# First attention of a four-layer MetaFormer: bias inside the score matmul, compact probabilities, product with V in 32x32 tiles

## The reference

```python
# 16 consecutive tokens form one sequence; 3 heads of 32 channels
qkv = x @ Wqkv + bqkv
q, k, v = jnp.split(qkv, 3, axis=-1)
q = q.reshape(B, G, P, H, DH) * SCALE
attn = jnp.einsum('bgihd,bgjhd->bghij', q, k)
bias = rel_table[REL_IDX].reshape(P, P, H).transpose(2, 0, 1)
attn = jax.nn.softmax(attn + bias[None, None], axis=-1)
out = jnp.einsum('bghij,bgjhd->bgihd', attn, v)
return out.reshape(B, G, P, D) @ Wm + bm
```

## Time and profile before

| what | value |
|---|---|
| runs | 892.6, 896.56, 895.98 us, median 895.98 |
| profiled execution | span 887.6 us; its own total time is not listed apart from the runs |
| TensorE busy | 789.4 us, 89% of the span |
| VectorE, GpSimd, ScalarE busy | 636.2, 563.9, 436.3 us |
| chain that ended last, whole program | TensorE 75%, VectorE 13%, issue 4%, ScalarE 3%, GpSimd 3% |
| steady part of the first attention | about 47 to 87 us of the span |

### The profile page before, as it was taken

The page is one execution under the profiler, slowest core; times in us unless marked ns, Lnnn a source line. Parts: engine busy times, 40 slices in busy tenths (PEclk is TensorE's granted clock), DMA queues, the critical chain, the costliest instruction groups (busy, mean ns, idle before and its releaser), DMA issues.

```text
span 887.6 us, 25193 instructions
## 1 busy us (share of the span) xinstructions
PE 789.4 (89%) x9360; PEld 647.9 (73%) x9360; DVE 636.2 (72%) x1699; ACT 436.3 (49%) x793; POOL 563.9 (64%) x887
## 2 busy tenths in 40 slices
PE   4778677579989999997998899999979998999996
PEld 4567465557867888885887678888868786888886
DVE  5899788658866777785778357777867774577755
ACT  1345355157755544435787354454545554445341
POOL 6443642345428788776876467887766776688765
PEclk9898778779999999998999899999988999999999
DMA  8610100000022110100001001101000001111030
GB/s 185 116 26 0 46 1 1 1 1 2 1 66 61 30 54 27 29 2 1 2 0 46 27 28 28 55 27 28 3 1 2 0 20 35 30 44 40 27 82 19
DMA packets 39515, 26.45 MB, mean 30 GB/s; under 512 B 27464, under 2 KB 32313, under 8 KB 39377
## 3 DMA queue, kind: packets, MB, share of 16 engines
q1 hardware_dynamic: 38428, 24.46, 11.0%
q10 hardware_dynamic: 998, 0.80, 0.4%
HBM read 8.33 MB, written 1.57 MB: 11 GB/s over the span
## 4 chain that ended last, share of the span: by engine, by line
PE 75%; DVE 13%; issue 4%; ACT 3%; POOL 3%; DMA 1%; ACTq 0%; DVEq 0%; POOLq 0%
PE PS L1580 21%; PE PS L1553 9%; PE PS L1554 8%; PE PS L1557 4%; PE PS L1357 3%; PE PS L1668 3%; PE PS L1655 2%; PE PS L1679 2%; PE PS L1343 2%; PE PS L1688 2%; PE PS L1345 2%; PE PS L1344 2%; PE PS L1490 2%; PE PS L1404 2%; PE PS L1698 2%
## 5 line engine op out<-in xcount | busy, mean ns | idle before, releaser
L667 ACT ACTIVATE H<-PS,B 128x512 f32<-128x512 f32 x288 | 173.7, 690 | 194.1 <-PE PS L1557 194.1
L1580 PEld LDWEIGHTS PS<-M,H 128*64 128x64 f32 x4608 | 192.3, 137 | 21.8 <-issue 15.1
L1580 PE MATMUL PS<-M,H 128*64 128x96 f32 x4608 | 205.2, 248 | 1.8 <-DVE X L1161 1.8
L1161 DVE SCALAR_TENSOR_TENSOR X<-PS,G,X 128x96 f32<-128x96 f32 (+1 forms) x384 | 121.8, 318 | 95.7 <-PE PS L1580 85.2
L465 POOL TENSOR_TENSOR msum<-stats 128x4 f32<-128x4 f32 (+1 forms) x61 | 16.0, 263 | 164.4 <-DVE stats L844 136.4
L1553 PE MATMUL PS<-XH,M1h 128*128 128x512 f32 x192 | 78.5, 409 | 0.0
L475 POOL TENSOR_TENSOR XN<-X,mean 128x384 f32<-128x384 f32 x56 | 47.1, 841 | 49.0 <-PE PS L1357 49.0
L1554 PE MATMUL PS<-FHL,M1l 128*128 128x512 f32 x192 | 76.9, 401 | 0.0
L501 POOL TENSOR_TENSOR PF<-G,B 128x1536 f32<-128x1536 f32 x24 | 66.2, 2760 | 10.2 <-DVE G L1152 10.2
L509 POOL TENSOR_TENSOR ex<-euler,dl 128x16 f32<-128x16 f32 x24 | 69.9, 2911 | 1.7 <-DVE dl L1125 1.6
L479 POOL TENSOR_TENSOR rs<-ve,half 128x4 f32<-128x4 f32 (+1 forms) x61 | 65.5, 1073 | 4.8
(11 more groups left out here) (248 smaller groups left out, 1902.7 us busy)
## 6 DMA issues: line engine op xcount, KB each, us to landing
FHL<-XH SPq DMA_DIRECT2D x36, 192.0 KB, 2.5
FHL<-XL SPq DMA_DIRECT2D x36, 64.0 KB, 2.1
X<-XH SPq DMA_DIRECT2D x12, 192.0 KB, 2.5
raw<-L_ffn_w SPq DMA_DIRECT2D x3, 576.0 KB, 4.8
M<-L_ffn_w SPq DMA_DIRECT2D x3, 576.0 KB, 6.0
X<-x SPq DMA_DIRECT2D x4, 384.0 KB, 7.9
XH<-XL SPq DMA_DIRECT2D x24, 64.0 KB, 1.9
out<-X SPq DMA_DIRECT2D x8, 192.0 KB, 2.6
```

The source lines that it names most:

```text
L667: act.activation(H[p][:, c, :], bank(UB[c]), ACT.Gelu, bias=B1[e][:, c:c + 1]).then_inc(gelu_a, 1)
L1161: ins = dve.scalar_tensor_tensor(xt(g, t), bank(4 + t % 2)[:, e * C:(e + 1) * C], G[:, t, e:e + 1], xt(g, t), ALU.mult, ALU.add)
L1580: ins = pe.matmul(Y[rows, x * C:(x + 1) * C], H[p][:, j, t * P + rows.start:t * P + rows.stop], M2[e][:, j, :], start=c == 0, stop=c == CH ...
```

## The change

- The rows 96 to 127 of qT and kT, zero before, hold an identity and the bias with the mask. The score matmul adds bias and mask itself; VectorE's addition (line 894) goes, and maximum and subtraction read PSUM. Two copies on VectorE fill these rows in the opening, and qT's are zeroed again after the phase.
- The probabilities are transposed by one 128-row instruction in place of four of 32 rows and stay compact (PA shrinks; its zeroing on GpSimd goes).
- The product with V is 48 matmuls of 32 keys by 32 channels by 32 tokens in place of 12; the keys of block q write bank q (0 to 3), and one ScalarE copy gathers the four banks.
- Banks: scores from 3 to 5, k from 1 to 4, V from 2 to 6 (shared with the output projection), and q stays in bank 0, which the product now uses too. So k comes first, q waits until OT has been copied, and V waits for the residual update of group g-1. ScalarE copies kT ahead of qT.
- In `body(7)` the product waits until the first feed-forward group has been read from banks 0 and 1, and `ffn_up(0)` waits for the OT copy of group 7.

```diff
-        PA = [hflat[1][:, o:o + HEADS * GTOK].rearrange("p (h t) -> p h t", h=HEADS) for o in (3072, 4608)]
+        PA = [hflat[1][:, o:o + GT * HEADS * 32] for o in (3072, 3456)]
...
+        KB, VB = (4, 1), (6, 2)
...
-                return PS[:, 3:4, 0:GT * HEADS * 32].rearrange("p b (u t h j) -> p (b u) t h j", u=2, t=2, h=HEADS)
+                return PS[:, 5:6, 0:GT * HEADS * 32].rearrange("p b (u t h j) -> p (b u) t h j", u=2, t=2, h=HEADS)
...
             for i in range(2):
-                ins = pool.memset(PA[i], 0.0)
-            ins.then_inc(ms_p, 1)
...
-                        act.activation(OT[0:C, :], bank(5, 512, C), ACT.Copy).then_inc(ot_a, 1)
+                        if ka == 1:
+                            act.activation(OT[0:C, :], bank(5, 512, C), ACT.Copy).then_inc(ot_a, 1)
+                        else:
+                            act.activation(OT[0:C, :].rearrange("c (t q j) -> c q t j", t=GT, q=4),
+                                           PS[0:C, 0:4, 0:GTOK // 4].rearrange("c q (t j) -> c q t j", t=GT), ACT.Copy).then_inc(ot_a, 1)
...
+                        dve.tensor_reduce(mx[:].rearrange("p (u v) -> p u v", u=2), S, AX.X, ALU.max).then_inc(mx_v, 1)
+                        dve.wait_ge(mx_v, n + 2)
                         if ka == 0:
                             after(dve, tr_v, g + 1)
-                            dve.tensor_tensor(sct, scores(0).rearrange("p u t h j -> p (u t) h j"),
-                                              BI[:].unsqueeze(1).to_broadcast([P, GT, HEADS, bs]), ALU.add).then_inc(sc_r, 1)
...
-                            for q in range(P // bs):
-                                rows = slice(q * bs, (q + 1) * bs)
-                                ins = dve.transpose(PA[1 - p][rows, :, :].rearrange("p h (t j) -> p t h j", t=GT)[:, :, :, rows],
-                                                    sct[rows])
-                            ins.then_inc(tr_v, 1)
+                            dve.transpose(PA[1 - p], SC[:, 0:GT * HEADS * bs]).then_inc(tr_v, 1)
...
+            dve.tensor_copy(qT[C:P, :].rearrange("p (r j) -> p r j", j=32), ident[C:P, C:P].unsqueeze(1).to_broadcast([P - C, GTOK // 32, 32]))
+            dve.tensor_copy(kT[C:P].rearrange("p h (r j) -> p h r j", j=32),
+                            BI[C:P].unsqueeze(2).to_broadcast([P - C, HEADS, GTOK // 32, 32])).then_inc(bias_v, 1)
...
             dve.wait_ge(xu[0], GROUPS)
-            dve.wait_ge(ms_p, 6)
+            dve.wait_ge(s_pe, GROUPS)
+            dve.memset(qT[C:P, :], 0.0).then_inc(ms_v, 1)
+            dve.wait_ge(ms_p, 5)
...
+                        elif isinstance(g, int) and g == GROUPS - 1:
+                            pe.wait_ge(fl_v, 1)
...
+                                for q in range(P // bs):
+                                    keys = slice(q * bs, (q + 1) * bs)
+                                    for h in range(HEADS):
+                                        rows = slice(h * DH, (h + 1) * DH)
+                                        ins = pe.matmul(PS[rows, q, t * bs:(t + 1) * bs], V[keys, t, rows],
+                                                        PA[p][keys, (t * HEADS + h) * bs:(t * HEADS + h + 1) * bs], start=True, stop=True)
...
+                        three(bank(KB[ka], 512, C), wh[:, C:2 * C], wl[:, C:2 * C], xh[:], xl[:]).then_inc(k_pe, 1)
+                        if ka == 0:
+                            if has(g, 0):
+                                pe.wait_ge(ot_a, n + 1)
+                            three(bank(0, 512, C), wh[:, 0:C], wl[:, 0:C], xh[:], xl[:]).then_inc(q_pe, 1)
...
+                        if ka == 0 and has(g, -1):
+                            pe.wait_ge(xu[0], g)
...
                         pe.wait_ge(wt_v, 7)
+                        pe.wait_ge(ot_a, GROUPS)
```

More of the change, by code:

```diff
@@ L549, in _ @@
             for i in range(2):
-                ins = pool.memset(PA[i], 0.0)
-            ins.then_inc(ms_p, 1)
-            for i in range(2):
                 pool.memset(BW[i][:], 0.0)
@@ L627, in body @@
                             rows = slice(h * DH, (h + 1) * DH)
-                            ins = act.activation(kT[rows, h, :], PS[rows, 1, :], ACT.Copy)
+                            ins = act.activation(kT[rows, h, :], PS[rows, KB[ka], :], ACT.Copy)
                         ins.then_inc(k_a, 1)
+                        if ka == 0:
+                            act.wait_ge(q_pe, n + 3)
+                            act.activation(qT[0:C, :], bank(0, 512, C), ACT.Copy, scale=QSCALE).then_inc(q_a, 1)
                     if has(g, 1):
                         act.wait_ge(xt_used, m + 2)
-                        act.activation(V[:].rearrange("p t c -> p (t c)"), bank(2, GT * C), ACT.Copy).then_inc(v_a, 1)
+                        act.activation(V[:].rearrange("p t c -> p (t c)"), bank(VB[ka], GT * C), ACT.Copy).then_inc(v_a, 1)
                     if has(g, 3, 2, PREPS[phase]):
@@ L970, in _ @@
             dve.memset(FL[C:P].bitcast(F32), 0.0)
-            dve.memset(kT, 0.0).then_inc(ms_v, 1)
+            dve.memset(kT[0:C], 0.0).then_inc(ms_v, 1)
             prep_lo(1, 1)
@@ L1363, in weight_sums @@
                 pe.matmul(PS[:, 3, 0:FG], onesf[0:C, :], gsum[0:C, 0:FG], start=True, stop=True)
-                pe.matmul(PS[:, 4, 0:FG], onesf[:], gsum2[:, 0:FG], start=True, stop=True).then_inc(wt_pe, 1)
+                pe.matmul(PS[:, 3, 16:16 + FG], onesf[:], gsum2[:, 0:FG], start=True, stop=True).then_inc(wt_pe, 1)
                 pe.wait_ge(wt_v, 5)
@@ L1400, in body @@
                             pe.wait_ge(sub_v, n + 1)
+                        if isinstance(g, int) and g == -1:
+                            if ka == 0:
+                                pe.wait_ge(bias_v, 3)
+                            else:
+                                pe.wait_ge(ms_v, 4)
                         for t in range(GT):
@@ L1429, in body @@
                             pe.wait_ge(pt_a, 3 * g + 3)
-                        weights = PT if ka == 1 else PA[p]
-                        after(pe, ot_a, n)
+                        elif isinstance(g, int) and g == GROUPS - 1:
+                            pe.wait_ge(fl_v, 1)
+                        if not has(g, -1):
+                            after(pe, ot_a, n)
                         for t in range(GT):
[L1433 to L1438, removed]
+                            if ka == 1:
+                                for h in range(HEADS):
+                                    rows = slice(h * DH, (h + 1) * DH)
+                                    o = PS[rows, 5, t * P:(t + 1) * P].rearrange("p (r h c) -> p h r c", h=2, r=8)
+                                    ins = pe.matmul(o, V[:, t, rows], PT[:, h, t * P:(t + 1) * P], start=True, stop=True)
+                            else:
+                                for q in range(P // bs):
+                                    keys = slice(q * bs, (q + 1) * bs)
+                                    for h in range(HEADS):
+                                        rows = slice(h * DH, (h + 1) * DH)
+                                        ins = pe.matmul(PS[rows, q, t * bs:(t + 1) * bs], V[keys, t, rows],
+                                                        PA[p][keys, (t * HEADS + h) * bs:(t * HEADS + h + 1) * bs], start=True, stop=True)
                         ins.then_inc(pv_pe, 1)
@@ L1448, in body @@
                         xh, xl = XH[1 - p], XL[1 - p]
+                        if ka == 0 and has(g, -1):
+                            pe.wait_ge(xu[0], g)
                         for t in range(GT):
                             ts = slice(t * P, (t + 1) * P)
-                            ins = three(PS[:, 2, t * C:(t + 1) * C], xh[:, ts], xl[:, ts], wh[:, 2 * C:], wl[:, 2 * C:])
+                            ins = three(PS[:, VB[ka], t * C:(t + 1) * C], xh[:, ts], xl[:, ts], wh[:, 2 * C:], wl[:, 2 * C:])
                         ins.then_inc(xt_used, 1)
```

24 lines of the change are left out of this document (8 added, 16 removed).

## The result

The first set of runs gave 878.59 us for the changed kernel (877.26 to 881.28, 4 runs) and 894.29 for the kernel before (891.38 to 896.56, 4 runs), a ratio of 0.9849 with a 95% interval of 0.9813 to 0.9886. Two later sets gave 0.9887 (0.9853 to 0.9921) and 0.9872 (0.9841 to 0.9903). All executions of each kernel together, on several chips, have their median at 892.0 us before (61 runs, 885.5 to 896.6) and 880.2 after (16 runs, 876.4 to 882.9). So the change saves about 11.8 us, 1.3%, where 9.35 was forecast; the first set showed 15.7.

A forecast was written before the change was run, and what follows sets the result against it. VectorE was taken to bound the first attention. Statistics 9.75 us earlier (four periods of 6.6 from 46.3, then the last chain) less 0.4 for the closing gave 9.35: median 895.98 to 886.6 us, range 883.0 to 893.5.

The forecast's parts named there:

- Bound and mechanism: First attention: VectorE sets the pace at 8.41 us a group; relieved of work, the stage ends earlier and the program wins that.
- the hand-over: Start of the first feed-forward group's statistics on VectorE, after the first attention: forecast at 77.8 instead of 87.55 us.
- VectorE's need: VectorE's work for one group of the first attention: 5.6 us after the change, 7.9 with upper bounds for transpose and subtraction.
- The product at 1.0 us: Product with V on TensorE, 96 records per group: 1.0 us, as before the change, bounds 0.7 and 2.6.
- The slow-product rival: Product with V at 20 to 27 ns a record costs 2.0 to 2.6 us; program at 890.3 to 893.2; chance 0.15.
- The period of 6.6: Time per group in the first attention: 6.6 us, lower bound 6.2 from TensorE's work alone; four periods follow group 2's scores.
- The opening at 0.3: Two copies on VectorE, about 1.3 us, mostly hidden in 1.72 us idle; 0.3 on the path, group 2's scores at 46.3.
- The closing at a cost of 0.4: End of the first attention: about 1.5 us of waits and a memset, mostly covered by TensorE's idle time; 0.4 on the path.
- the one from the difference to the time: Whole program: a gain of 9.35 us takes the span from 887.6 to about 878.2 and the median from 895.98 to 886.6.
- The clock rival: TensorE, now the bound, pays clock dips in full, 3 us for a 6 us dip; program at 889.6 to 892.6; chance 0.12.
- The slower rival: Product with V without load and stream overlapping, 55 ns a record: 5.3 us, period 10.5, program about 906.7; chance 0.05.
- a gain that is not passed on: Feed-forward phase waits for something attention does not set, such as a weight transfer; time stays near 895; chance 0.06.

The follow-up runs named there:

- the four transposes: Changed kernel with its one 128-row transpose split again into four of 32 rows: ratio 0.9937 to the kernel before, period 6.77 us.
- head by head: Changed kernel with the same 48 matmuls of the product with V reordered, 32 records in a row in one channel strip: ratio 0.9844 to the kernel before.
- late copies: Changed kernel with both opening copies moved behind the zeroing of W2B: ratios 0.9870 and 0.9841 to the kernel before, median 878.8 us against 880.2.
- doubled product: Changed kernel with each of the 48 matmuls of the product with V issued twice: ratio 1.0220 to the kernel before.

## Why the prediction was right and wrong

- **Bound and mechanism: right.** VectorE set the pace, the loop through OT and q does now, and the gain arises at the hand-over. The addition and the transposes had the forecast price, 0.58 and 1.74 us. So had the subtraction, 0.56. VectorE's need came out lower than the 5.6 us forecast, at 5.0 (the 6.77 of the four transposes less 1.74), since the normalisation got faster too; that was slack. Two slips in the working change nothing: with both upper bounds VectorE's need is 7.8 us and not 7.9, and 1.47/6 is 0.245 us and not 0.23.
- **The product at 1.0 us: right in size, wrong in reason.** It takes 0.95. The prediction took it from weights that load side by side in three strips at 28 ns; head by head it would then have cost 2.7, and it cost the same. By the Trainium skill's figure of about 25 ns between starts ("TensorE: Matmul & The Clock Gate", Part 1, "Wait — 56ns, not 53.3ns?") it would have been an estimated 2.4. The runs don't agree: they show 10 ns a record on average, less than half of the figure, and 20 ns for a matmul of two records. The slow-product rival falls with it.
- **The period of 6.6: too long by 0.4.** The loop was named rightly (XL, subtraction, exponential, OT, q). Its terms were too generous: V was read to the end of its last record, 1.44 instead of 1.27 to the start of the next work, the transposes at 0.69 instead of 0.56, and 0.15 added for semaphores that the durations held already. The lower bound of 6.2, TensorE's work alone, had the same fault: it is 5.95. Four periods took 24.83 us (46.86 to 71.69) instead of 26.4, 1.6 less.
- **The opening at 0.3: too cheap.** The scores of group 2 start at 46.86 instead of the 46.3 of the forecast. The copies took 2.16 us instead of 1.3, and the idle time that was to hide them moved with them. The late copies recover 1.5 us at the hand-over.
- **Those two give the hand-over:** 77.8 - 1.6 + 0.56 = 76.8, against 76.71.
- **The closing at a cost of 0.4: wrong in sign.** It won about 1.0 us (11.8 at the second turn against 10.8 at the hand-over). The reason is open.
- **The step that failed most is the one from the difference to the time.** 886.6 stood on one median of three runs, 895.98, and on a distance of 8.4 us between span and median that was taken as fixed. The distance is 1.8 us in one and the same execution; the rest was spread. The kernel's runs spread over 11 us with the granted clock of stages that the change doesn't touch; over 61 runs their median is 892.0. So the start of the sum was 4.0 us too high, and from 892.0 the forecast difference would have given 882.6.
- **What is left.** The first set's 878.59 lies 8.0 us below 886.6: 4.0 from the median of before, 2.4 from the change (1.0 in the stage and 1.4 in the closing, from 882.6 to the pooled 880.2), and 1.6 from the spread of four runs. The split of the 2.4 is read from five profiles; the error of the pooled means (before 891.6 with a deviation of 3.2, after 879.9 with 2.3) is about 0.7 us on the difference. The pooled 880.2 is also below the range, by 2.8. The range reached 7 us to the slow side and 3.6 to the fast, though the spread of runs alone asks for more than that.
- **The clock rival:** did not occur in the changed kernel (1.00 in each window of the stage, in three profiles), but the doubled product shows that it is near. The slower rival and the one of a gain that is not passed on did not occur either.

## What to carry to other kernels

When a step is to be hidden in an engine's idle time, ask what that idle time waits for, and whether the step stands ahead of something that this other engine needs: then it moves the idle time and is not hidden by it. When the pace passes from one engine to another, look for the loop through all of them, and read each term from start to start. An engine that is busy 99% of a period need not be its bound: here 0.22 us of waiting were hidden behind the ends of matmuls. And forecast a difference by the stage's own hand-over, then give the time a range that holds the spread of the runs.

## What was unexpected of the hardware

- Matmuls of 32x32x32 in float32 leave TensorE at an average of 10 ns a record (96 in 0.95 us, 192 in about 2.0), in both orders tried and with each matmul issued twice in a row.
- On VectorE a subtraction of two SBUF operands grew from 0.56 to 1.12 us beside GpSimd's wide steps; with one operand in PSUM it stayed at 0.56 beside them.
- A stream transpose costs 0.58 us for 384 elements in a row, over 32 rows or over 128.
- A copy of 1536 elements with a repeated source takes 1.74 us on 32 rows, where the cast of as many on 96 took 0.94. The copy of 512 elements repeats its source too and took 0.42, so the repetition alone is not the reason; it stays open.
- With the product issued twice, TensorE stopped for up to 2.42 us inside its own work, each time until 1.3 to 1.5 us after a 16 KB packet on the instruction queue had landed. That the stops wait for instructions is likely and not proven.
